# Attention values of a macaron block made in two halves next to fills of transposes

## Chip, core and metric

The kernel runs on one core of a Trainium2 chip. The metric is the device time of one execution in microseconds (us), as the median of several runs. The core's engines are PE (TensorE, the matrix engine), PEld (PE's weight loads, which overlap its matmuls), DVE (VectorE), ACT (ScalarE), POOL (GpSimd) and SP (SyncE, which issues the DMAs here). Each follows its own list of instructions in order and waits on semaphores.

## What is computed

Eight sequences of 512 tokens with 256 channels go through half a feed-forward network, attention with 16 heads of 16 channels and a distance bias, and the same half network again. Everything is float32.

```python
x = x + 0.5 * ffn(layernorm(x))      # silu(x @ wg.T) * (x @ wu.T) @ wd.T, hidden 768
x = x + attention(layernorm(x))
x = x + 0.5 * ffn(layernorm(x))
# attention: B, L, C, H = 8, 512, 256, 16; D = 16
scores = einsum('bhld,bhsd->bhls', qh, kh) * D ** -0.5 - slope[h] * |l - s|
attn = softmax(scores, axis=-1)
out = einsum('bhls,bhsd->bhld', attn, vh)   # then @ Wo.T + bo
```

## The kernel before

There are three stages, each over all eight sequences: the first feed-forward half, attention, and the second half. In the profiled execution attention runs from about 199 to 687 us. The change touches attention alone.

**Steps.** Attention of a sequence b is written out as 4 quads (n = 0 to 3, four heads each) of 8 steps (s = 0 to 7), so 256 steps in all; "step (n, s)" names one. A step deals with one block of 128 keys and one pair of heads. PE makes two score tiles of 512 queries each (`scores`, out of weights `k_aug` and moving `q_aug`), ACT takes the exponential of both at once into `probs` (L656), and POOL multiplies the diagonal block by a table (L525). In every even step PE also makes *values*: `weigh_values` (L1156) multiplies the `probs` of a finished key block, four heads at once in four column strips of 32, with `v_aug` and adds them up in the bank `pv`. The block that an even step takes is two key blocks back, since `probs` has two buffers. The exponentials of an even step go into the buffer which that step's values read, so ACT waits for both `st_done` (the second score tile) and `pv_done` (the values).

**Maxima tiles.** The softmax needs each row's maximum ahead of time. PE makes scores a second time in the other orientation (`scores_for_max`, weights `q_aug`, moving `k_aug`), 64 tiles a sequence, two in each step and 26 tiles ahead, and DVE reduces each (`row_max`, L837). The tiles go in turn to two banks, so a tile waits (`s1_used`) until DVE is through with the tile two before it. A score tile and a maxima tile use different halves of PE's rows. After 16 tiles DVE makes the negated maxima of a quad in two small operations (`max_in`, L847 and L849), and PE transposes them in a later "max" fill; a DMA then brings them to `q_aug`. Where a sequence's list is at its end (the last sequence from step (2, 3) on) there are no tiles.

**Fills.** Every odd step and every step (n, 4) carries a *fill*, a piece of the work on the sequence before, this one or the next, by the table `FILLS`: 8 of the 16 odd steps have four 128-column transposes (`xt`, `turn`, `heads`), the others 6 or 12 matmuls of a projection (`qk`, `v`, `out`), and each (n, 4) the transposes of the maxima. ACT copies a fill's bank to `stage` (L600, L603) or `v_new`, and a next fill waits for that copy. For some of them ACT rounds the copy (L621) and DVE (L893, for `xt`, two steps later) or POOL (L481, for `qk` and `turn`) makes the remainder. DVE also divides the heads (L901, L903), applies layernorms (`apply_kept`, L726) and does the first steps of the last layernorm. All of this stands in each engine's list between the row maxima.

**PE's order in a step** (`turn`): first score tile, first maxima tile, then in an even step the max fill (if s is 4) and the values, in an odd step the fill, then second score tile, second maxima tile. The first score tile of a step waits for the exponentials of two steps before (`exp_done`), whose banks it takes.

## Time and profile before

| | us |
|---|---|
| median of 3 runs | 855.21 (854.73 to 856.42) |
| the profiled execution, device time | 849.82 |
| its span, first to last instruction | 847.9 |
| PE busy | 792.2 (93%) |
| DVE busy | 659.4 (78%) |
| ACT busy | 510.3 (60%) |
| POOL busy | 428.1 (50%) |

Starts of instructions are measured; the ends of matmuls are modelled, and successive matmuls overlap. So PE is read by the distance between starts, not by its busy time. A merged row of the timeline gives the start of the first of its instructions, the time until the last one ends, and their number; two instructions of one engine with the same names stand in one row when nothing else of that engine stands between them. Values are x8 in the trace for four instructions of the program, each of which runs as two.

### The profile page before, as it was taken

To read this page: it belongs to the slowest core of one execution; us is meant where nothing else is said; L and a number is where in the kernel's file an instruction comes from. 1 tells how busy PE (TensorE), PEld (TensorE's weight loads), DVE (VectorE), ACT (ScalarE), POOL (GpSimd) and SP (SyncE) were. 2 spreads that over 40 slices of the span, in tenths; PEclk is the share of its full clock that TensorE was granted. 3 is DMA by queue.
4 is the path that set the end of the run, shared out by engine and by line. 5 is a ranking of instruction groups with operands and counts; after the bars stand their busy time and mean duration, and the time that the engine had idled before them with its cause. 6 is when DMAs were issued, how large, how long until landed. Compare 5 with 4: busy or idle time off the path is not lost.

```text
span 847.9 us, 13038 instructions
## 1 busy us (share of the span) xinstructions
PE 792.2 (93%) x4576; PEld 494.2 (58%) x4576; DVE 659.4 (78%) x1347; ACT 510.3 (60%) x745; POOL 428.1 (50%) x486
## 2 busy tenths in 40 slices
PE   2699999999999999999999999999999799999997
PEld 2478888765444454444454454454453367878886
DVE  6489877977899878978978878878888537677764
ACT  4244354334776877877767777768777774444433
POOL 0244344434564665755755666665664454444433
PEclk9799999998999999999999999999999999999999
DMA  9330005503540540640730720621520000000001
GB/s 362 127 42 3 2 17 78 59 3 43 75 70 9 82 70 3 97 56 2 108 45 7 109 39 19 97 39 32 84 39 2 2 2 27 26 27 28 27 27 51
DMA packets 21491, 43.18 MB, mean 51 GB/s; under 512 B 3848, under 2 KB 5912, under 8 KB 21208
## 3 DMA queue, kind: packets, MB, share of 16 engines
q1 hardware_dynamic: 21400, 41.92, 26.8%
q8 instruction: 63, 1.03, 0.6%
q14 instruction: 28, 0.23, 0.1%
HBM read 12.02 MB, written 4.62 MB: 20 GB/s over the span
## 4 chain that ended last, share of the span: by engine, by line
PE 76%; DVE 17%; issue 3%; DMA 2%; SPq 1%; ACT 1%; DVEq 0%; ACTq 0%
PE ps L970 70%; DVE row_max L837 6%; DVE hid L771 3%; PE ps L1033 2%; DMA q_scale<-q_scale 2%; PE ps L982 1%; DVE max_in L847 1%; DVE max_in L849 1%; DVE newton L703 1%; PE ps L1028 1%; DVE rstd L705 1%; PE ps L1038 1%; PE ps L1008 1%; DVE newton L701 1%; SPq L365 1%
## 5 line engine op out<-in xcount | busy, mean ns | idle before, releaser
L837 DVE TENSOR_REDUCE row_max<-ps 128x1 f32<-128x512 f32 x512 | 331.5, 685 | 72.5 <-PE ps L970 71.6
L656 ACT ACTIVATE probs<-ps 128x1024 f32<-128x1024 f32 x256 | 262.6, 1030 | 84.1 <-PE ps L970 83.3
L525 POOL TENSOR_TENSOR probs<-probs,diag 128x256 f32<-128x256 f32 x256 | 187.8, 734 | 207.2 <-ACT probs L656 205.7
L457 POOL TENSOR_TENSOR hid_r<-hid,hid_r 128x512 fp32r<-128x512 f32 x96 | 124.8, 1301 | 191.0 <-ACT hid_r L551 190.2
L970 PE MATMUL ps<-k_aug,q_aug 60*128 60x512 f32 x512 | 209.8, 470 | 10.9 <-DVE row_max L837 10.2
L970 PE MATMUL ps<-xnt,wgu_r 128*128 128x512 f32 x768 | 193.9, 406 | 18.7 <-DVE hid L771 14.4
L970 PE MATMUL ps<-q_aug,k_aug 62*128 62x512 f32 x512 | 193.4, 454 | 2.7 <-ACT probs L656 2.7
L970 PEld LDWEIGHTS ps<-xnt,wgu_r 128*128 128x128 f32 x768 | 144.2, 192 | 59.6 <-DVE hid L771 19.8
L970 PEld LDWEIGHTS ps<-q_aug,k_aug 62*128 62x128 f32 x512 | 80.6, 186 | 141.7 <-issue 123.9
L970 PE MATMUL ps<-probs,v_aug 128*32 128x512 f32 x1024 | 137.1, 608 | 0.0
L557 ACT ACTIVATE gated<-ps 128x512 f32<-128x512 f32 x96 | 57.3, 598 | 131.2 <-PE ps L970 121.8
L970 PEld LDWEIGHTS ps<-k_aug,q_aug 60*128 60x128 f32 x512 | 84.7, 185 | 40.6 <-DVE row_max L837 30.3
L771 DVE SCALAR_TENSOR_TENSOR hid<-ps,gated 128x512 f32<-128x512 f32 x96 | 65.8, 687 | 46.4 <-ACT gated L557 23.9
L970 PE MATMUL ps<-wdn_r,hid_r 128*128 128x256 f32 x768 | 97.6, 283 | 2.3 <-ACT stage L603 2.3
L970 PEld LDWEIGHTS ps<-wdn_r,hid_r 128*128 128x128 f32 x768 | 93.5, 188 | 5.2 <-ACT hid_r L551 3.2
L551 ACT CAST hid_r<-hid 128x512 fp32r<-128x512 f32 x96 | 59.0, 615 | 24.3 <-DVE hid L771 24.3
L603 ACT COPY stage<-ps 128x512 f32<-128x512 f32 x96 | 56.2, 585 | 20.6 <-PE ps L970 15.7
L970 PE MATMUL ps<-xnt,wqkv 128*128 128x512 f32 x168 | 46.6, 412 | 0.0
L481 POOL TENSOR_TENSOR parts<-stage,parts 128x512 fp32r<-128x512 f32 x32 | 41.3, 1292 | 0.0
L970 PEld LDWEIGHTS ps<-probs,v_aug 128*32 128x32 f32 x1024 | 20.2, 108 | 32.0 <-issue 24.5
L675 DVE BATCH_NORM_STATS2 stats<-x_sb 128x6 f32<-128x256 f32 x96 | 34.1, 409 | 5.3 <-DMA x_sb<-x_in 5.3
L712 DVE TENSOR_SCALAR xn<-x_sb,mean_var,rstd 128x256 f32<-128x256 f32 x64 | 37.7, 614 | 0.5
(72 smaller groups left out, 670.7 us busy)
## 6 DMA issues: line engine op xcount, KB each, us to landing
q_aug<-parts SPq DMA_DIRECT2D x96, 128.0 KB, 4.5
k_aug<-parts SPq DMA_DIRECT2D x96, 128.0 KB, 4.7
x_sb<-x_in SPq DMA_DIRECT2D x8, 512.0 KB, 12.9
x_out<-x_sb SPq DMA_DIRECT2D x8, 512.0 KB, 2.6
diag<-diag_table SPq DMA_DIRECT2D x1, 2048.0 KB, 18.8
wgu_i<-w_gate_up SPq DMA_DIRECT2D x2, 768.0 KB, 6.1
w_att<-w_att SPq DMA_DIRECT2D x1, 1024.0 KB, 11.3
q_aug<-max_row SPq DMA_DIRECT2D x64, 8.0 KB
```

The source lines that it names most:

```text
L457: nc.gpsimd.tensor_tensor(hid_r[:, 1, f, :], hid[:, f % 2, :], hid_r[:, 0, f, :].bitcast(F32), ALU.subtract).then_inc(s["hid_lo"], 1)
L481: nc.gpsimd.tensor_tensor(lo, stage[:, slot_of(b, name), :], hi.bitcast(F32), ALU.subtract).then_inc(done[SPLIT_POOL], 1)
L525: nc.gpsimd.tensor_tensor(tile, tile, diag[:, kt % 2, n * QH + 2 * pair:n * QH + 2 * pair + 2, :], ALU.mult).then_inc(fixed, 1)
L551: nc.scalar.copy(hid_r[:, 0, f, :], hid[:, f % 2, :]).then_inc(s["hid_hi"], 1)
L557: nc.scalar.activation(gated[:, f % 2, :], ps[:, gate_at + f % 2, :], ACT.Silu, scale=DEQ).then_inc(s["gated_ready"], 1)
L603: nc.scalar.copy(stage[:, slot_of(b, name), :], bank).then_inc(drained, 1)
L656: nc.scalar.activation(probs[:, kt % 2, 2 * pair:2 * pair + 2, :], ps[:, at:at + 2, :], ACT.Exp, scale=SLOPE_UNITS[pair]).then_inc(exp_don ...
L675: nc.vector.bn_stats(stats[:, slot, tile, :], x_of(b, tile)).then_inc(ln_step, 1)
L712: nc.vector.tensor_scalar(xn[:, tile, :], x_of(b, tile), mean_var[:, 0, tile, 0:1], rstd[:, 0, tile:tile + 1], ALU.subtract, ALU.mult).the ...
L771: nc.vector.scalar_tensor_tensor(hid[:, f % 2, :], ps[:, up_at + f % 2, :], DEQ, gated[:, f % 2, :], ALU.mult, ALU.mult).then_inc(s["hid_r ...
L837: nc.vector.reduce_max(row_max[:, quad % 2, i, pair, t:t + 1], max_bank(tile), mybir.AxisListType.X).then_inc(s1_used, 1)
L970: return nc.tensor.matmul(out, lhs, rhs, start=start, stop=stop, **k)
```

## The change

An even step that has maxima tiles and whose next step carries a fill of transposes by the table (`xt`, `turn` or `heads`) now makes its values in two parts. Queries 0 to 255 of all four heads come where the values stood. Then come the second score tile and the second maxima tile. Queries 256 to 511 follow after them, at the end of the step, and `pv_done` is raised by these alone. The bank is opened for accumulation by the first part of a quad's first block. These are steps 0, 2 and 4 of quad 0, steps 0 and 4 of quads 1 and 2, and step 4 of quad 3. In the first sequence two of the eight have no values, in the last one two have no tiles, so 60 steps are split. Other engines' programs are the same.

```diff
+TURNS = ("xt", "turn", "heads")
...
-            def weigh_values(quad_no, quad, kt, seq):
+            def weigh_values(quad_no, quad, kt, seq, cols=((0, L),)):
...
-                for g in range(QH):
-                    ins = matmul(pv[32 * g:32 * g + 32, :], v_aug[:, kt, quad * QH + g, :], probs[:, kt % 2, g, :],
-                                 kt == 0, kt == TT - 1, skip_group_check=True)
-                ins.then_inc(pv_done, 1)
+                for lo, hi in cols:
+                    for g in range(QH):
+                        ins = matmul(pv[32 * g:32 * g + 32, lo:hi], v_aug[:, kt, quad * QH + g, :],
+                                     probs[:, kt % 2, g, lo:hi], kt == 0 and lo == 0, kt == TT - 1, skip_group_check=True)
+                if cols[-1][1] == L:
+                    ins.then_inc(pv_done, 1)
...
+                            in_halves = tiles and FILLS[n, s + 1].startswith(TURNS)
                             if s >= 4:
-                                weigh_values(quad_no, n, (s - 4) // 2, b)
+                                values = (quad_no, n, (s - 4) // 2, b)
                             elif not (first(b) and n == 0):
-                                weigh_values(quad_no - 1, (n - 1) % NQ, s // 2 + 2, b)
+                                values = (quad_no - 1, (n - 1) % NQ, s // 2 + 2, b)
+                            else:
+                                values = ()
+                            if values:
+                                weigh_values(*values, ((0, L // 2),) if in_halves else ((0, L),))
...
                         if tiles:
                             scores(b, n, s, 1).then_inc(st_done, 1)
                         scores_for_max(b, tiles[1:])
+                        if s % 2 == 0 and in_halves and values:
+                            weigh_values(*values, ((L // 2, L),))
```

The first place is PE's list at step (1, 0) and the start of step (1, 1) of a sequence. Scores are printed as `ps<-q_aug,k_aug`, maxima tiles as `ps<-k_aug,q_aug`, values as `ps<-probs,v_aug`. Before:

```order
L970 MATMUL ps<-k_aug_86,q_aug_61 128x512 [waits s1_used]
L970 MATMUL ps<-probs,v_aug 32x512 [waits fixed]
L970 MATMUL ps<-probs,v_aug 32x512 x3
L970 MATMUL ps<-q_aug_61,k_aug_86 128x512
L970 MATMUL ps<-k_aug_86,q_aug_61 128x512 [waits s1_used]
L970 MATMUL ps<-q_aug_61,k_aug_86 128x512 [waits exp_done]
L970 MATMUL ps<-k_aug_86,q_aug_61 128x512 [waits s1_used]
L1038 MATMUL ps<-eye,heads 128x128 [waits heads_done,drained]
```

And now:

```order
L972 MATMUL ps<-probs,v_aug 32x256 x3
L972 MATMUL ps<-q_aug_61,k_aug_86 128x512
L972 MATMUL ps<-k_aug_86,q_aug_61 128x512 [waits s1_used]
L972 MATMUL ps<-probs,v_aug 32x256 [waits fixed]
L972 MATMUL ps<-probs,v_aug 32x256 x3
L972 MATMUL ps<-q_aug_61,k_aug_86 128x512 [waits exp_done]
L972 MATMUL ps<-k_aug_86,q_aug_61 128x512 [waits s1_used]
L1040 MATMUL ps<-eye,heads 128x128 [waits heads_done,drained]
```

The four matmuls of 512 columns have become two groups of four with 256, and the second group stands between the second maxima tile of the step and the first score tile of the next.

The second place is PE's list at step (0, 4), from the maxima's transposes to the first of step (0, 5). Before:

```order
L1028 MATMUL ps<-eye,max_in 32x128 [waits neg_ready,drained]
L970 MATMUL ps<-probs,v_aug 32x512 [waits heads_t_ready,v_ready,fixed]
L970 MATMUL ps<-probs,v_aug 32x512 x3
L970 MATMUL ps<-q_aug_60,k_aug_64 128x512
L970 MATMUL ps<-k_aug_86,q_aug_61 128x512 [waits s1_used]
L970 MATMUL ps<-q_aug_60,k_aug_64 128x512 [waits exp_done]
```

And now:

```order
L1030 MATMUL ps<-eye,max_in 32x128 [waits neg_ready,drained]
L972 MATMUL ps<-probs,v_aug 32x256 [waits heads_t_ready,v_ready,fixed]
L972 MATMUL ps<-probs,v_aug 32x256 x3
L972 MATMUL ps<-q_aug_60,k_aug_64 128x512
L972 MATMUL ps<-k_aug_86,q_aug_61 128x512 [waits s1_used]
L972 MATMUL ps<-probs,v_aug 32x256 [waits heads_t_ready,v_ready,fixed]
L972 MATMUL ps<-probs,v_aug 32x256 x3
L972 MATMUL ps<-q_aug_60,k_aug_64 128x512 [waits exp_done]
```

The same split stands behind the transposes of the maxima, whose own waits have not moved.

## Rows read from the trace of the kernel before

**Rows 1.** The page's part 4: the chain that ended last, by line.
```profile
PE ps L970 70%; DVE row_max L837 6%; DVE hid L771 3%; PE ps L1033 2%; DMA q_scale<-q_scale 2%; PE ps L982 1%; DVE max_in L847 1%; DVE max_in L849 1%; DVE newton L703 1%; PE ps L1028 1%; DVE rstd L705 1%; PE ps L1038 1%; PE ps L1008 1%; DVE newton L701 1%; SPq L365 1%
```
**Rows 2.** Busy time of each engine in sequences 1 to 5 (PE, PEld, DVE, ACT, POOL).
```profile
261.00:570.00 309.00, 304.68 (x1826) 149.41 (x1828) 258.60 (x432) 231.97 (x321) 188.10 (x241) 1.00 0.36 53
```
**Rows 3.** Timeline of PE, sequence 3, steps (1, 0) to (1, 2): start, time, instruction.
```profile
399.48 0.40 PE L970 MATMUL ps<-q_aug,k_aug 62*128 62x512 f32 x1
399.81 1.06 PE L970 MATMUL ps<-probs,v_aug 128*32 128x512 f32 x8
400.80 0.49 PE L970 MATMUL ps<-q_aug,k_aug 62*128 62x512 f32 x1
...
401.14 0.39 PE L970 MATMUL ps<-q_aug,k_aug 62*128 62x512 f32 x1
401.48 0.66 PE L1038 MATMUL ps<-eye,heads 128*128 128x128 f32 x4
402.06 0.49 PE L970 MATMUL ps<-q_aug,k_aug 62*128 62x512 f32 x1
...
402.45 0.46 PE L970 MATMUL ps<-q_aug,k_aug 62*128 62x512 f32 x1
402.71 0.50 PE L970 MATMUL ps<-k_aug,q_aug 60*128 60x512 f32 x1
403.14 1.07 PE L970 MATMUL ps<-probs,v_aug 128*32 128x512 f32 x8
...
404.48 0.40 PE L970 MATMUL ps<-q_aug,k_aug 62*128 62x512 f32 x1
```
**Rows 4.** The same timeline, the second four of the values from 399.81 alone.
```profile
400.26 0.61 PE L970 MATMUL ps<-probs,v_aug 128*32 128x512 f32 x4
```
**Rows 5.** Timeline of DVE beside rows 3.
```profile
399.71 1.29 DVE L837 TENSOR_REDUCE row_max<-ps 128x1 f32<-128x512 f32 x2 [0.75 <-PE ps L970]
401.37 2.57 DVE L837 TENSOR_REDUCE row_max<-ps 128x1 f32<-128x512 f32 x4 [0.37 <-PE ps L970]
```
**Rows 6.** Timeline of DVE, sequence 3, steps (0, 5) and (0, 6).
```profile
393.51 1.29 DVE L837 TENSOR_REDUCE row_max<-ps 128x1 f32<-128x512 f32 x2 [0.43 <-PE ps L970]
394.72 1.14 DVE L893 TENSOR_TENSOR xnt<-stage,xnt 128x512 fp32r<-128x512 f32 x1
395.78 2.56 DVE L837 TENSOR_REDUCE row_max<-ps 128x1 f32<-128x512 f32 x4
```
**Rows 7.** Timeline of ACT at step (0, 5), which starts at 393.29.
```profile
393.48 1.02 ACT L656 ACTIVATE probs<-ps 128x1024 f32<-128x1024 f32 x1 [0.44 <-PE ps L970]
```
**Rows 8.** Timeline of POOL behind it.
```profile
394.58 0.72 POOL L525 TENSOR_TENSOR probs<-probs,diag 128x256 f32<-128x256 f32 x1 [0.95 <-ACT probs L656]
```
**Rows 9.** Timeline of PE at the end of step (0, 6).
```profile
396.28 0.49 PE L970 MATMUL ps<-q_aug,k_aug 62*128 62x512 f32 x1
396.51 0.50 PE L970 MATMUL ps<-k_aug,q_aug 60*128 60x512 f32 x1
```
**Rows 10.** Timeline of DVE in the first stage, two small operations.
```profile
81.94 0.16 DVE L719 TENSOR_SCALAR kept_mean<-mean_var 128x4 f32<-128x4 f32 x1
82.01 1.28 DVE L719 TENSOR_SCALAR kept_rstd<-rstd 128x4 f32<-128x4 f32 x1
```
**Rows 11.** Timeline of POOL beside them.
```profile
81.98 1.28 POOL L457 TENSOR_TENSOR hid_r<-hid,hid_r 128x512 fp32r<-128x512 f32 x1
```
**Rows 12.** Timeline of DVE, sequence 3, steps (1, 3) and (1, 4).
```profile
405.43 0.48 DVE L847 TENSOR_SCALAR max_in<-row_max 128x16 fp32r<-128x16 f32 x1
...
408.40 0.58 DVE L726 TENSOR_SCALAR xn<-x_sb,kept_mean,kept_rstd 128x256 f32<-128x256 f32 x1
```
**Rows 13.** Timeline of POOL beside rows 12.
```profile
404.52 1.34 POOL L481 TENSOR_TENSOR att_t<-stage,att_t 128x512 fp32r<-128x512 f32 x1
...
408.78 1.33 POOL L481 TENSOR_TENSOR parts<-stage,parts 128x512 fp32r<-128x512 f32 x1
```
**Rows 14.** Timeline of PE, sequence 3, step (2, 4).
```profile
422.98 0.50 PE L970 MATMUL ps<-k_aug,q_aug 60*128 60x512 f32 x1 [0.50 <-DVE row_max L837]
```

## The prediction

> **What bounds the kernel now.** I read the chain of waits first: 70% of the span lies on PE's matmuls, and the row maxima of DVE hold 6%, the largest share of another engine's line [rows 1]. The busy times of sequences 1 to 5 say the same: in 309 us PE is busy 304.7, DVE 258.6, ACT 232.0, POOL 188.1 [rows 2]. A sequence takes 309/5 = 61.8 us. PE's busy time hides short waits, so I went to the distances between starts, in a step pair that the change touches [rows 3].
>
> Step (1, 0) runs freely. First score tile to values is 0.33 us (399.48 to 399.81), values to second score tile 0.99 (to 400.80), and from there to the next step 0.34: 1.66 in all. The transposes of step (1, 1) take 0.58 (401.48 to 402.06), and with two tile pairs of 0.335 that step would last 1.25. It lasts 1.31 (401.14 to 402.45), since its second maxima tile comes 0.05 late. Step (1, 2) lasts 2.03 (to 404.48) where 1.66 was free: its first maxima tile starts at 402.71, 0.26 behind its score tile, and the values stand 0.43 behind that tile, not 0.33.
>
> DVE explains this [rows 5]. Four row maxima in one run take 2.57 us, so they stand (2.57 - 0.69)/3, about 0.62 us, apart, and a bank is free 0.74 after its row maximum starts. The tiles come unevenly: two within 0.34 us around each step's border, and none for 1.33 while values run. DVE is idle 0.37 before the run and then cannot keep up with four tiles in a row. The wait behind transposes is thus one of rhythm. 8 steps of a sequence are like (1, 1). Free work adds up to about 56 us a sequence (16 even steps of 1.66, four transposes of maxima at 0.3, 16 pairs of tile pairs, and the fills), so waits are about 5.7.
>
> **The split itself.** The second four of the values start 0.45 behind the first (399.81 to 400.26, [rows 4]), and the next tile 0.54 behind them [rows 3]. 512 columns in two passes at 2.4 GHz are 0.427, so 0.026 and 0.115 are not streaming. A half costs 0.213 + 0.026 + 0.213 + 0.115 = 0.57, two halves 1.14 against 0.99. That is **+0.14 us in each of 60 steps, +8.5 us**, all on PE's path. No row shows a 256-column half. Below, the bound is proportion: 0.50 a half and nothing added. Above, I take the first transpose in rows 3, which costs about 0.06 more than the others (0.58 for four at about 0.11, plus the drain): with that at every half it is 0.63, +0.26 a step, +15.8 us. I take 0.57, since all its terms stand around the same instructions.
>
> The split has four changes between tile pairs and values where there were two. I charge one more, since two tile pairs that follow each other also stand 0.34 apart (400.80 to 401.14), 0.12 above 512 columns [rows 3]: the change in front of values costs nothing that a tile pair would not. The Trainium skill, in "TensorEngine Tiling (Array Packing)", section "Key Properties", says that changing the tiling mode drains TensorE, whatever comes next. By that rule two changes are new, with the row's 0.115 each an estimate of +0.26 a step, and the whole change would bring about 1 us; that time is rival D's.
>
> **What the halves give back.** With 0.57 the tiles of a split step come at 0, 0.90, of the next at 1.87, 2.79, of the one after at 3.12. I followed DVE's queue: a row maximum starts 0.56 after its tile's start or 0.61 after the one before; a tile waits until 0.74 after the start of the one two before. Then step (1, 0) lasts 1.875 (its second maxima tile waits 0.07 for a bank), step (1, 1) 1.25, step (1, 2) 1.725 (first maxima tile 0.055 late). Sum 4.85 against 5.00: **a gain of 0.14 to 0.15**, made of -0.22, +0.06 and +0.30. Beside (n, 4) in quad 3 the bank wait is absent and it is 0.23.
>
> ACT's exponential of a split step now waits for the second half. In PE's trace values end modelled 1.06 after their start, 0.07 behind the next score tile's start; ACT starts some 0.04 later, 0.11 into the next step, where it was 0.19 [rows 7]. Its 1.03 us end at 1.14, before step (1, 2) wants the bank at 1.25. No cost, with 0.07 to spare.
>
> **Give-backs, quad by quad.** *Quad 1*: at (1, 3) and (1, 4) POOL holds DVE up. The small `max_in` takes 0.48 where it needs 0.17, until POOL's operation ends at 405.86 [rows 12, 13]. POOL follows ACT, which moves little, so the 0.30 won at (1, 2) comes back at (1, 4) as 0.28 (its first maxima tile 0.80 late, not 0.52). With two gains of 0.15 and 0.22, I get +0.08. *Quad 2*: POOL is without a gap from (2, 1) to (2, 4); the maxima tile at 422.98 stands 0.89 into its step [rows 14], and keeps its absolute place. +0.21. *Quad 3*: +0.23. *Quad 0*: (0, 0) to (0, 2) are even (4.99 before and after). Step (0, 4) gets 0.24 longer: `xnt` (L893) of step (0, 3) is asked for at 1.30, POOL's multiplication starts at 1.21, and DVE stays behind it as now. Step (0, 5) gains 0.06. There the second `xnt` takes 1.14 us today, from 394.72, because POOL began at 394.58 [rows 6, 8], and the next row maximum slips to 395.78; PE's second maxima tile at (0, 6) starts 0.23 behind its score tile [rows 9] and 0.25 more are lost in (0, 7). After the change DVE has no backlog: row maximum at 0.565, `xnt` at 1.165, and POOL at 0.11 + 1.10 = 1.21 (exponential to POOL is 1.10 in rows 7 and 8). DVE is first by 0.05, and steps (0, 6) and (0, 7) come to 1.725 and 2.27 in place of 2.25 and 2.62. Quad 0: **+0.75**.
>
> A sequence wins 0.75 + 0.08 + 0.21 + 0.23 = 1.27; five of them 6.35. Sequence 6 is busier on DVE behind quad 0: 0.9. Sequence 7, tiles until (2, 2): 0.4. Sequence 0, without three of the transposes: 0.4. **Sum: -8.1 us**, net of the +8.5. From the profiled execution, 849.8, that gives 841.7. The runs' median is 5.4 above that execution, and I subtract from the median: **847.1 us**.
>
> **Rivals.** *A. POOL is first at (0, 5).* Its lead is decided by 0.05 us, from distances each good to 0.03. For DVE first: the operation at 81.94 ran in 0.16 though POOL started 0.04 behind it, while the one at 82.01, 0.03 behind POOL, took 1.28 [rows 10, 11]. So the earlier start wins, by whatever margin. Against: recorded starts of DVE overlap the instruction before by 0.08. Then quad 0 gives -0.12, a sequence 0.40, the whole about -2.6: 852.6 us. The Trainium skill, in "SBUF — State Buffer", section "Who interferes with whom", has the same rule: issue order decides, the second fully blocks, and a DVE operation with two SBUF inputs counts. By it the price is this one and no partial slowing.
>
> *B. A dear half.* The split costs more than it gives back. Each of 60 steps gives (8.1 + 8.5)/60 = 0.28 us before its cost, so the result turns slower from a half of 0.64 on (0.50 + 0.14). At 0.66, as if each half paid the 0.06 of a first transpose and the drain of a change at both ends, it is +0.18 a half-pair over my sum, +11: 858 us. For it: no row has column strips of 256. Against: the fixed terms in rows 3 and 4 are measured on these strips.
>
> *C. Two missed gaps.* A, and at (1, 4) the layernorm `xn` (L726) misses the gap between POOL's two operations. Today it is asked for at 408.40, and POOL's next, of 1.33, starts at 408.78 [rows 12, 13]; I put the request 0.10 ahead of that start. If missed, DVE waits 1.3 and 0.66 of the gain in (1, 5) and (1, 6) goes. A sequence then loses 0.26, the whole about 1.5: 856.7 us, measured the same or slower.
>
> *D. The change does little*: with two new drains, a half of 0.63, its effects nearly cancel, 8.1 - 60 x 0.115 = 1.2 us faster: 854.0. Against it stand the equal distances of rows 3.
>
> **How the numbers follow.** Forecast 0.42; A 0.24; B 0.11; C 0.11; D 0.12. A measurement of this kernel can tell about 0.2%, 1.7 us, from no change. Faster by more: the forecast, most of A (0.21) = 0.63, and a little of C's weaker form 0.02: 0.65. Within: 0.12 + 0.03 + 0.05 = 0.20. Slower: 0.11 + 0.04 = 0.15. Range: at its low end the forecast with a half of 0.54 (3.6 us less), 843.5; at its high end A and D and the mild form of C, 856.5.
>
> **What would show it.** In the profile after: (1) distance between the two starts of a half and the score tile behind it, 0.57; (2) steps (1, 0), (1, 1), (1, 2) of 1.87, 1.25, 1.73; (3) exponential of a split step 0.11 into the next; (4) at (0, 5) `xnt` in about 0.6 us and POOL's multiplication behind it, steps (0, 6) and (0, 7) of 1.73 and 2.27; (5) the first maxima tile of (1, 4) about 0.80 late; (6) a sequence of about 60.5 us. Wrong would be a half above 0.64, or `xnt` still at 1.1 us in (0, 5), or PE waiting for `exp_done` behind the transposes.

## Result: the changed kernel is slower

| | before | after |
|---|---|---|
| median, us | 855.21 (854.73 to 856.42) | 864.33 (863.43 to 865.05) |
| ratio after/before, 95% interval | | 1.0116 [1.0087, 1.0145] |
| profiled execution / its span, us | 849.82 / 847.9 | 864.14 / 862.4 |
| granted clock of PE, mean over the span | 0.990 | 0.974 |

The change costs 1.2%. The forecast was 847.1 us with a range of 843.5 to 856.5: wrong in sign, and the time is outside the range. Two executions far above all others are in no median: one of the kernel before (1718 us) and one of the run `q0_fed` below (1054 us, mean granted clock 0.644).

From the profile of the changed kernel, the busy us and share by engine, and the granted clock in 40 slices, in tenths:

```profile
PE 801.2 (93%) x5056; PEld 499.4 (58%) x5056; DVE 662.7 (77%) x1347; ACT 511.4 (59%) x745; POOL 434.1 (50%) x486
PEclk9799999997998999999999999999999799999999
```

The chain that ended last has hardly changed: PE's matmuls hold 69% of it and the row maxima 5%, against 70% and 6% in [rows 1]. The row of clocks has three dips inside attention (slices 10, 13 and 32, counted from 1) where before's profiled execution has one. (The dip in slice 2 stands in the first feed-forward half, in both kernels.) Next, the busy times by stretch (window, length, busy us of PE, PEld, DVE, ACT, POOL with counts; granted clock, DMA share, GB/s). The stretches are sequence 0, sequences 1 to 5, sequence 6, and sequence 7 to the last step. Before:

```profile
198.60:260.60 62.00, 58.82 (x314) 27.23 (x313) 53.64 (x111) 42.00 (x56) 30.75 (x41) 0.94 0.48 67
260.60:569.40 308.80, 304.48 (x1821) 149.57 (x1822) 258.45 (x433) 231.77 (x320) 188.04 (x241) 1.00 0.36 53
569.40:632.70 63.30, 62.34 (x366) 30.92 (x365) 54.42 (x107) 46.79 (x65) 37.70 (x49) 1.00 0.35 52
632.70:685.30 52.60, 46.41 (x277) 19.20 (x273) 31.41 (x55) 39.49 (x52) 27.89 (x37) 1.00 0.01 2
```

After:

```profile
198.70:266.40 67.70, 63.74 (x361) 28.91 (x361) 53.71 (x111) 42.17 (x56) 30.72 (x41) 0.85 0.43 61
266.40:576.20 309.80, 303.16 (x2143) 151.55 (x2142) 261.56 (x433) 232.54 (x320) 192.28 (x241) 1.00 0.35 53
576.20:640.40 64.20, 62.10 (x432) 31.04 (x428) 55.08 (x107) 46.64 (x65) 38.53 (x49) 1.00 0.35 51
640.40:698.70 58.30, 52.00 (x325) 20.64 (x321) 31.84 (x55) 39.56 (x52) 28.68 (x37) 0.88 0.01 2
```

The 14.5 us between the two profiled spans are +5.7 in sequence 0, +1.0 in sequences 1 to 5, +0.9 in sequence 6, +5.7 in sequence 7 and +1.2 outside. So there are two separate results. Sequences 1 to 5 run at full clock in both and lose 1.0 us where 6.35 were to be won. Sequences 0 and 7 hold 12 of the 60 split steps and lose 11.4 us, with the granted clock down from 0.94 to 0.85 and from 1.00 to 0.88.

**Inside a step.** The timeline of PE in sequence 3, steps (1, 0) to (1, 2) of the changed kernel (start, time, instruction, count; compare [rows 3]):

```profile
405.74 0.39 PE L972 MATMUL ps<-q_aug,k_aug 62*128 62x512 f32 x1
406.06 0.64 PE L972 MATMUL ps<-probs,v_aug 128*32 128x256 f32 x8
406.63 0.49 PE L972 MATMUL ps<-q_aug,k_aug 62*128 62x512 f32 x1
406.71 0.49 PE L972 MATMUL ps<-k_aug,q_aug 60*128 60x512 f32 x1
407.13 0.64 PE L972 MATMUL ps<-probs,v_aug 128*32 128x256 f32 x8
407.70 0.50 PE L972 MATMUL ps<-q_aug,k_aug 62*128 62x512 f32 x1
...
408.13 0.66 PE L1040 MATMUL ps<-eye,heads 128*128 128x128 f32 x4
408.71 0.50 PE L972 MATMUL ps<-q_aug,k_aug 62*128 62x512 f32 x1
...
409.06 0.42 PE L972 MATMUL ps<-q_aug,k_aug 62*128 62x512 f32 x1
...
410.75 0.39 PE L972 MATMUL ps<-q_aug,k_aug 62*128 62x512 f32 x1
```

A half takes 0.57 (406.06 to 406.63, 407.13 to 407.70), as forecast. The three steps last 1.96, 1.36 and 1.70, 5.02 together, against 4.85 forecast and 5.00 before. What is longer than forecast is a tile pair that stands alone between two blocks of other work. From the second tile of the pair to the second half are 0.42 (406.71 to 407.13), from the pair of step (1, 1) to the transposes 0.43 (407.70 to 408.13). Both were charged 0.335. No wait is behind this, as steps (3, 4) and (3, 5) of the same sequence show, where the maxima tile starts with its score tile:

```profile
446.52 0.50 PE L972 MATMUL ps<-q_aug,k_aug 62*128 62x512 f32 x1
446.52 0.50 PE L972 MATMUL ps<-k_aug,q_aug 60*128 60x512 f32 x1
446.95 0.64 PE L972 MATMUL ps<-probs,v_aug 128*32 128x256 f32 x8
447.52 0.50 PE L972 MATMUL ps<-q_aug,k_aug 62*128 62x512 f32 x1
447.52 0.49 PE L972 MATMUL ps<-k_aug,q_aug 60*128 60x512 f32 x1
447.95 0.66 PE L1035 MATMUL ps<-eye,heads_t 128*128 128x128 f32 x4
```

Two lone pairs, 0.43 each, both tiles starting together. In the kernel before, as long as there are maxima tiles, a pair always has another behind or ahead of it, and the two take 0.68 together (400.80 to 401.48 in [rows 3]). Where the second of two pairs has its maxima tile late (402.71), from that tile to the values are 0.43 as well: the prediction read that row as rhythm. The end of the last sequence has no maxima tiles, and there the kernel before has lone pairs, of two score tiles. They take 0.43 too:

```profile
672.24 0.50 PE L970 MATMUL ps<-q_aug,k_aug 62*128 62x512 f32 x2
672.67 1.07 PE L970 MATMUL ps<-probs,v_aug 128*32 128x512 f32 x8
```

**What a lone pair pays for.** 0.43 us would be 512 columns in two passes at 2.4 GHz, so a lone pair might simply stream that long. The trace of the kernel before says no. Six matmuls of 512 columns of a projection fill, declared with the same data type as the tiles (`F32R`), take 1.58 from the first to the next score tile:

```profile
404.81 1.65 PE L970 MATMUL ps<-xnt,wqkv 128*128 128x512 f32 x6
406.39 0.49 PE L970 MATMUL ps<-q_aug,k_aug 62*128 62x512 f32 x1
```

One takes 0.43, two in a row 0.67 to 0.68, six 1.58: 0.23 to 0.25 for each one more, and about 0.2 once for the whole run. 0.213 is one pass of 512 columns at 2.4 GHz. At half clock (rows of sequence 7 of the changed kernel) a lone pair takes 0.72 and two in a row 1.15:

```profile
665.58 0.79 PE L972 MATMUL ps<-q_aug,k_aug 62*128 62x512 f32 x1
666.30 1.11 PE L1035 MATMUL ps<-eye,heads_t 128*128 128x128 f32 x4
667.35 0.79 PE L972 MATMUL ps<-q_aug,k_aug 62*128 62x512 f32 x1
...
668.50 1.93 PE L972 MATMUL ps<-probs,v_aug 128*32 128x512 f32 x8
```

The second pair adds 0.43, which is one pass at 1.2 GHz, while two passes would make the lone pair 0.85. So the tiles stream once, and some 0.2 us (0.3 at half clock) are paid once for every unbroken run, at its ends. Where one kind of matmul follows another and both use the whole array, in the first stage, no such price shows. The next row counts the last four of a 512-column projection, and the kind behind them starts 0.94 later, 0.235 for each of the four:

```profile
60.38 1.10 PE L970 MATMUL ps<-xnt,wgu_r 128*128 128x512 f32 x4
61.32 0.28 PE L970 MATMUL ps<-wdn_r,hid_r 128*128 128x256 f32 x1
```

In 20 of the 22 changes between two projections in that stage the distances are like that. A single maxima tile between two projections takes 0.42 to 0.43 there in all 12 places, though its data type is theirs. The price thus goes with the change between the whole array and a part of it, and a split adds one run of tiles and one of values. (A change to transposes, which are of another data type, adds about 0.1 in that stage without a change of tiling, so the data type may hold a part of the price beside values or transposes.)

**Quad by quad.** Sequence 3, from the start of each quad's first step, in us:

| quad | before | after | change | forecast | forecast + 0.19 for each split step |
|---|---|---|---|---|---|
| 0 (3 split steps) | 15.16 | 14.79 | -0.37 | -0.75 | -0.18 |
| 1 (2) | 15.33 | 16.00 | +0.67 | -0.08 | +0.30 |
| 2 (2) | 15.75 | 15.67 | -0.08 | -0.21 | +0.17 |
| 3 (1) | 15.46 | 15.44 | -0.02 | -0.23 | -0.04 |

The last column adds two lone pairs of 0.43 - 0.335 = 0.095 to each split step. It accounts for quad 3. Quads 0 and 2 come out about 0.2 better than it, quad 1 is 0.37 worse. That the four together fit, +0.20 measured and +0.25 in the last column, is partly luck. The reason for quad 1 stands in DVE's timeline at step (1, 4):

```profile
414.96 1.52 DVE L728 TENSOR_SCALAR xn<-x_sb,kept_mean,kept_rstd 128x256 f32<-128x256 f32 x1
```

and in POOL's beside it:

```profile
415.05 1.28 POOL L483 TENSOR_TENSOR parts<-stage,parts 128x512 fp32r<-128x512 f32 x1
```

The layernorm `xn` starts at 414.96, 0.09 (from unrounded starts 0.084) ahead of POOL's `parts` at 415.05, takes 1.52 and ends 0.15 behind it. In [rows 12] it took 0.58, and POOL's operation started 0.38 behind it [rows 13]. In sequence 4 of the same execution it came through:

```profile
476.87 0.41 DVE L728 TENSOR_SCALAR xn<-x_sb,kept_mean,kept_rstd 128x256 f32<-128x256 f32 x1
```
```profile
476.97 1.44 POOL L483 TENSOR_TENSOR parts<-stage,parts 128x512 fp32r<-128x512 f32 x1
```

The recorded lead is 0.10 there. It is 0.08 in the four sequences that missed, and 0.07 to 0.09 in the five of run `mid` below, which all missed. Quad 1 took 15.62 in the sequence that came through and 16.00 to 16.03 in 1, 2, 3 and 5. So to be first in the records is not enough; with a single one that came through, where the border lies isn't known.

At (0, 5) DVE is first, as the forecast had it:

```profile
401.44 0.68 DVE L895 TENSOR_TENSOR xnt<-stage,xnt 128x512 fp32r<-128x512 f32 x1
```

POOL's multiplication follows at 401.58, and the operation takes 0.68 in place of 1.14 [rows 6].

**The clock.** PE in sequence 7, steps (1, 3) and (1, 4) of the changed kernel:

```profile
661.07 0.46 PE L972 MATMUL ps<-q_aug,k_aug 62*128 62x512 f32 x1
662.74 0.50 PE L972 MATMUL ps<-k_aug,q_aug 60*128 60x512 f32 x1 [1.22 <-DVE row_max L839]
...
664.57 1.08 PE L972 MATMUL ps<-probs,v_aug 128*32 128x256 f32 x8
```

And the busy times just before and after 664.1:

```profile
657.30:664.10 6.80, 5.22 (x35) 2.27 (x34) 5.84 (x9) 5.23 (x8) 4.10 (x5) 1.00 0.00 0
664.10:670.90 6.80, 6.80 (x30) 2.44 (x32) 2.67 (x4) 2.64 (x3) 1.45 (x2) 0.50 0.01 2
```

Sequence 7 has little beside its own steps: its list has no `qk` and `v` fills, and at (1, 4) PE waits for DVE. PE is busy 5.22 of 6.80 us, then the granted clock is 0.50 (1.2 GHz in place of 2.4), and the same eight matmuls of 256 columns take 1.08 where they took 0.64. Sequence 0, which has no `turn` or `heads` of a sequence before, has such stretches too. In the changed kernel's profiled execution attention holds four of them (from 203.3, 257.9, 664.1 and 681.2 us, 34 us together), in before's one, at 203.5, of 6.8 us. The Trainium skill's page "TensorE: Matmul & The Clock Gate" names the behaviour in its section "HAM oscillation — how this bites in real kernels"; it says that waits make the clock fall and that the work behind them starts slow, at a penalty of half the throttled time. This stretch agrees on the first, but waits alone don't decide it: in before's profiled execution PE is busy 15.56 of the 20 us from 660 us on, about the same share, and the clock stays at 1.00. On the second, an estimate by that page would be 0.5 us for each us at half clock; the executions below show 0.38.

**Half-clock time.** Each execution comes with its span and mean granted clock, so its time at half clock is 2 x (1 - clock) x span. That is 43 us for the changed kernel (41 to 45 in its four executions) and 17 in before's profiled one. It differs between executions of the same kernel, as the next section shows, and everything from here on is read with it.

### The profile page after: what moved, and what is told of

The parts are those of the page before. It is cut to its first block, busy times and chain, and to the rows that moved or that the text cites. A ratio compares the mean times of both kernels' runs of the same rounds, so it can differ in the third digit from the quotient of the medians.

```text
span 862.4 us, 14028 instructions
## 1 busy us (share of the span) xinstructions
PE 801.2 (93%) x5056; PEld 499.4 (58%) x5056; DVE 662.7 (77%) x1347; ACT 511.4 (59%) x745; POOL 434.1 (50%) x486
## 3 DMA queue, kind: packets, MB, share of 16 engines
q8 instruction: 66, 1.08, 0.6%
## 4 chain that ended last, share of the span: by engine, by line
PE 75%; DVE 15%; issue 4%; DMA 2%; ACT 2%; SPq 1%; DVEq 0%; ACTq 0%
PE ps L972 69%; DVE row_max L839 5%; DVE hid L773 3%; PE ps L1035 2%; DMA q_scale<-q_scale 2%; PE ps L984 1%; DVE newton L705 1%; DVE max_in L851 1%; DVE max_in L849 1%; PE ps L1040 1%; DVE xn L728 1%; PE ps L1030 1%; ACT probs L658 1%; DVE rstd L707 1%; PE ps L1010 1%
## 5 line engine op out<-in xcount | busy, mean ns | idle before, releaser
L839 DVE TENSOR_REDUCE row_max<-ps 128x1 f32<-128x512 f32 x512 | 335.9, 685 | 79.5 <-PE ps L972 78.3
L527 POOL TENSOR_TENSOR probs<-probs,diag 128x256 f32<-128x256 f32 x256 | 193.5, 756 | 214.8 <-ACT probs L658 213.0
L972 PE MATMUL ps<-k_aug,q_aug 60*128 60x512 f32 x512 | 214.8, 480 | 11.7 <-DVE row_max L839 11.6
L972 PE MATMUL ps<-q_aug,k_aug 62*128 62x512 f32 x512 | 206.7, 473 | 3.5 <-ACT probs L658 3.4
L972 PEld LDWEIGHTS ps<-q_aug,k_aug 62*128 62x128 f32 x512 | 85.3, 189 | 145.9 <-issue 129.0
L972 PE MATMUL ps<-probs,v_aug 128*32 128x256 f32 (+1 forms) x1504 | 154.7, 484 | 0.0
L972 PEld LDWEIGHTS ps<-k_aug,q_aug 60*128 60x128 f32 x512 | 89.4, 187 | 29.7 <-DVE row_max L839 26.2
L972 PEld LDWEIGHTS ps<-probs,v_aug 128*32 128x32 f32 x1504 | 29.9, 109 | 48.4 <-issue 39.5
## 6 DMA issues: line engine op xcount, KB each, us to landing
w_att<-w_att SPq DMA_DIRECT2D x1, 1024.0 KB, 10.7
```

The lines of the kernel that those rows point to most:

```text
L527: nc.gpsimd.tensor_tensor(tile, tile, diag[:, kt % 2, n * QH + 2 * pair:n * QH + 2 * pair + 2, :], ALU.mult).then_inc(fixed, 1)
L839: nc.vector.reduce_max(row_max[:, quad % 2, i, pair, t:t + 1], max_bank(tile), mybir.AxisListType.X).then_inc(s1_used, 1)
L972: return nc.tensor.matmul(out, lhs, rhs, start=start, stop=stop, **k)
```

## Experiments

The runs were made in three batches, each beside its own executions of the kernel before. "At 17" is the value at 17 us of half-clock time on a straight line through all executions of that kernel, time against half-clock time. The slopes of these lines are 0.19 to 0.44. With 0.38 for all, the values move by at most 1.4 us (`ends` 852.1, `end7` 850.5, `late` 870.7), so "at 17" is good to about 1 us.

| kernel | median us (range, executions) | half-clock us, median | at 17 | ratio to before, 95% |
|---|---|---|---|---|
| before, batch 1 | 854.18 (848.33 to 859.56, 35) | 22 | 851.3 | |
| same | 853.64 (847.44 to 857.5, 12) | 21 | 851.4 | 0.9984 [0.9949, 1.0019] |
| mid | 855.66 (850.59 to 859.82, 12) | 22 | 852.8 | 1.0003 [0.9969, 1.0036] |
| ends | 860.82 (851.96 to 862.9, 12) | 40 | 851.4 | 1.0053 [1.0021, 1.0085] |
| adjacent | 850.39 (848.66 to 857.14, 12) | 15 | 851.1 | 0.9961 [0.9934, 0.9989] |
| before, batch 2 | 853.74 (847.66 to 860.09, 29) | 20 | 851.1 | |
| after_fed | 861.74 (852.51 to 864.51, 11) | 34 | 855.3 | 1.0071 [1.0036, 1.0107] |
| before_fed | 849.28 (847.81 to 852.31, 12) | 10 | 850.8 | 0.9978 [0.9949, 1.0007] |
| mid_apply | 851.77 (848.49 to 857.63, 12) | 21 | 850.8 | 0.9995 [0.9961, 1.0029] |
| late | 879.20 (872.59 to 882.84, 3) | 39 | 869.4 | 1.0298 [1.0231, 1.0366] |
| before, batch 3 | 854.44 (848.84 to 857.51, 33) | 21 | 852.6 | |
| q0_fed | 847.89 (846.53 to 848.96, 9) | 15 | 848.3 | 0.9933 [0.9908, 0.9957] |
| end0 | 854.20 (850.29 to 860.63, 12) | 24 | 851.5 | 1.0013 [0.9985, 1.0040] |
| end7 | 854.85 (851.88 to 861.13, 12) | 31 | 851.9 | 1.0011 [0.9986, 1.0037] |
| adjacent_all | 851.58 (850.22 to 854.7, 12) | 18 | 851.7 | 0.9976 [0.9956, 0.9997] |

### The kernel before, beside itself

No edit: the kernel before under a name of its own.

> The kernel before, submitted against itself, to see the granted clock of each execution. Theory (half-clock stretches): an execution with clock 0.99 in the mean takes about 850 us, and those near 855 us show a lower mean clock, since 6.8 us at half speed on a busy PE cost about 3.4 us. Rival (the 5.4 us between the profiled execution and the median have nothing to do with PE's clock): clock 0.99 in all of them. Ratio 1.000 either way.

Its twelve executions run from 847.44 to 857.5 us, a spread of 1.2%. In order of half-clock time (us of time / us at half clock): 847.4/10, 848.1/10, 849.4/10, 849.5/10, 853.0/19, 854.3/19, 852.2/24, 855.6/26, 854.8/31, 856.7/32, 857.1/33, 857.5/33. The line has a slope of 0.36 us for each us at half clock (0.38 in before's 35 executions), and leaves 1.2 us (one standard deviation) unexplained. So most of this kernel's scatter goes with the clock. It also explains about half of the 5.4 us by which the profiled execution of before, 849.8, lay under its median of 855.2. It had 17 us at half clock, where 22 are usual and 39 the most, and the line is at 851.3 there, 2.9 under the median of the 35. Of the rest, 1.0 is that the median of the first three was high (854.2 in the 35), and 1.5 is scatter.

### Splits in the middle, splits at the ends

`mid` splits the 48 steps of sequences 1 to 6, `ends` the 12 of sequences 0 and 7.

```diff
-                            in_halves = tiles and FILLS[n, s + 1].startswith(TURNS)
+                            in_halves = tiles and FILLS[n, s + 1].startswith(TURNS) and 0 < b < B - 1
```
```diff
+                            in_halves = tiles and FILLS[n, s + 1].startswith(TURNS) and b in (0, B - 1)
```

> The split in sequences 1 to 6 alone, 48 steps. Theory (the loss is half-clock time in the first and last sequence, where fills are missing): those two are as before, sequences 1 to 5 take 0.2 us more each and sequence 6 about 0.9, so 1.5 to 2.5 us over the kernel before, with no half-clock stretch beyond its own. Rival (the split costs about the same in each of the 60 steps): 48/60 of 9.1, so 7.3 us over.

> The split in sequences 0 and 7 alone, 12 steps, the complement of the run before. Theory (half-clock time): 7 to 12 us over the kernel before, with four half-clock stretches in attention, 34 us in all. Rival (cost per step): 12/60 of 9.1, so 1.8 us over.

`ends` is the slower of the two with a quarter of the splits: +6.6 us by the medians. Nearly all of it comes with half-clock time, 40 us against 22. At equal half-clock time it is within 1 us of before (851.4 against 851.3). Its profiled execution has three low stretches in attention, not the four expected: before's one at 203 us and two more, of 6.8 and 13.6 us, both in sequence 7. Its stretch of sequence 7:

```profile
643.00:699.00 56.00, 50.61 (x281) 20.29 (x282) 25.67 (x46) 35.25 (x45) 25.82 (x33) 0.82 0.01 2
```

`mid` has before's half-clock time, and is 1.5 us slower at equal half-clock time. The medians differ by 1.5 too, though the ratio's interval holds 1. That is the 1.5 to 2.5 expected; 7.3 would lie outside the interval. In the profiles sequences 2 to 5 take 61.9 each, against 61.7. The low clock isn't confined to the two ends: the profiled execution of `mid` has a stretch of it in sequence 6, which before's has not, and quad 1 takes 19.20 there against 16.26 in the changed kernel:

```profile
571.00:638.00 67.00, 64.72 (x432) 31.66 (x428) 55.48 (x107) 46.78 (x65) 38.39 (x49) 0.95 0.32 49
```

### One end alone

```diff
+                            in_halves = tiles and FILLS[n, s + 1].startswith(TURNS) and b == 0
```
```diff
+                            in_halves = tiles and FILLS[n, s + 1].startswith(TURNS) and b == B - 1
```

> The split in sequence 0 alone (6 steps). Theory (clock): half-clock time rises over the kernel before's 20 to 22 us by what the changed kernel has more in sequence 0, up to 14 us, and the time goes along with 0.35 to 0.4 us for each: 855 to 860 us. Rival (steps in sequence 0 cost by themselves): 6 x 0.1 us, no more half-clock time.

> The split in sequence 7 alone (6 steps). Theory (clock): half-clock time rises by up to 14 us, 855 to 860 us, and together with end0 the two rises add up to that of run ends, 18 us in the median. Rival: no more half-clock time, 0 to 1 us slower.

Both medians, 854.20 and 854.85, stay under the 855 to 860 expected. The means rise by only 0.9 and 1.3 us over before's, those of `ends` by 5.9. Mean half-clock times rise by 5 and 7 us, those of `ends` by 13, so the clock's part about adds up. At the slope of 0.38 these are 2 and 3 us, and `end0` and `end7` come out about 1 us better at equal half-clock time than before in that batch. That before is itself 1.3 us higher at 17 than in the two other batches. I take this for the limit of what such comparisons settle, about 1 us.

### Values in two groups, but in one place

`adjacent` makes the two halves of the 60 steps one behind the other where values stood before. `adjacent_all` does so in every even step.

```diff
-                                weigh_values(*values, ((0, L // 2),) if in_halves else ((0, L),))
+                                weigh_values(*values, ((0, L // 2), (L // 2, L)) if in_halves else ((0, L),))
...
-                        if s % 2 == 0 and in_halves and values:
-                            weigh_values(*values, ((L // 2, L),))
```

> All 60 steps make values in two groups of 256 columns, but both where the values stood, with nothing between them. Theory (what costs is a lone pair of tiles between two changes of tiling, and the clock follows idle time, not short matmuls): values take 1.04 us instead of 0.995, PE's other distances are as before, no new half-clock stretch; 0 to 3 us over the kernel before. Rival (256 columns in strips are what costs): as the changed kernel, 9 us over.

> Values in two groups of 256 columns with nothing between them in all even steps, also those next to other fills (run adjacent had it in 60 steps, and had less half-clock time than the kernel before in its 12 executions, 15 against 22 us in the median). If twice as many, shorter matmuls keep the clock up, the half-clock time is again at 10 to 16 us and the time 849 to 851. If that was chance, 20 to 22 us and 854 again.

PE at step (1, 0) of `adjacent`:

```profile
399.14 1.07 PE L972 MATMUL ps<-probs,v_aug 128*32 128x256 f32 x16
400.14 0.50 PE L972 MATMUL ps<-q_aug,k_aug 62*128 62x512 f32 x1
```

1.00 for sixteen records of 256 columns against 0.99 for eight of 512 [rows 3]: less than the 1.04 expected. The width of the groups costs nothing; all that a split costs is in leaving and coming back. Both kernels stand within 1 us of their batch's before at equal half-clock time (851.1 against 851.3, 851.7 against 852.6), and yet their medians are 3.8 and 2.9 us under it, with 15 and 18 us at half clock. The 18 us and 851.6 of `adjacent_all` lie between the two cases of its expectation (10 to 16 us, or 20 to 22). That these kernels meet the low clock less often is measured, why is not known.

### Values whole, behind the second maxima tile

`late` makes the values of the 60 steps whole, in the place of the second half. Each split step then has three tile pairs on one side and one on the other.

```diff
-                            if values:
-                                weigh_values(*values, ((0, L // 2),) if in_halves else ((0, L),))
+                            if values and not in_halves:
+                                weigh_values(*values)
...
-                            weigh_values(*values, ((L // 2, L),))
+                            weigh_values(*values)
```

> In all 60 steps the values are made whole, behind the second maxima tile. Theory (a lone pair of tiles between two blocks of other tiling takes 0.43 us, two pairs in a row 0.67): values take 0.995 again, the pair in a split step costs 0.335 each, the pair between values and the transposes 0.43, so step (1, 0) is 1.66 and (1, 1) 1.36 us. Rival (the 0.43 belongs to 256-column groups): the pair behind whole values takes 0.335, step (1, 1) 1.25 to 1.31. For the time each expects about the kernel before, since DVE's tiles come in pairs again, plus the exponential's later start.

PE at steps (1, 0) and (1, 1):

```profile
408.93 0.49 PE L972 MATMUL ps<-k_aug,q_aug 60*128 60x512 f32 x1 [0.35 <-DVE row_max L839]
409.35 1.06 PE L972 MATMUL ps<-probs,v_aug 128*32 128x512 f32 x8
410.35 0.49 PE L972 MATMUL ps<-q_aug,k_aug 62*128 62x512 f32 x1
410.77 0.66 PE L1040 MATMUL ps<-eye,heads 128*128 128x128 f32 x4
```

The lone pair behind values takes 0.42 here too (410.35 to 410.77), though these values are whole: the price belongs to standing alone, not to halves. But step (1, 0) is 2.39 long, where 1.66 was expected. Three maxima tiles in a row meet two banks, and PE waits for DVE, 0.35 at the tile of 408.93. At equal half-clock time the kernel is about 18 us slower (three executions). My expectation had counted PE's instructions and not DVE's rhythm.

### The gap of `xn`

`mid` again, with the second part of the kept layernorm one step later.

```diff
-APPLY_AT = {(1, 2): 0, (1, 4): 1, (1, 6): 2, (2, 2): 3}
+APPLY_AT = {(1, 2): 0, (1, 5): 1, (1, 6): 2, (2, 2): 3}
```

> The split in sequences 1 to 6, as in run mid, with DVE's layernorm of one tile (line 728) moved from step (1, 4) to (1, 5). Theory (the missed gap between two POOL operations at (1, 4) costs quad 1 its 0.67): quad 1 of sequences 1 to 5 takes 15.3 to 15.4 us in place of 16.02, and the whole is 3 to 4 us under run mid at the same half-clock time. Rival (quad 1 loses by PE's extra time in its two split steps): quad 1 stays within 0.1 of 16.0.

DVE's `xn` in `mid`, then in `mid_apply`:

```profile
409.33 1.52 DVE L728 TENSOR_SCALAR xn<-x_sb,kept_mean,kept_rstd 128x256 f32<-128x256 f32 x1
```
```profile
410.76 0.41 DVE L728 TENSOR_SCALAR xn<-x_sb,kept_mean,kept_rstd 128x256 f32<-128x256 f32 x1
```

Quad 1 of sequence 3 goes from 16.04 to 15.62, of the others in the same way. So the missed gap costs 0.42 a sequence, not the 0.66 of rival C, and the quad doesn't come down to the 15.3 to 15.4 expected. The 0.29 left over before's 15.33 are what two split steps with their lone pairs come to in the table above (0.30). The whole comes 2.0 us under `mid` at equal half-clock time, under the 3 to 4 expected, though the two are of different batches. Five times 0.42 are 2.1: sequence 6 has no such layernorm, and its quad 1 takes 16.26 in `mid_apply` as in the changed kernel.

### Work that nobody reads

`before_fed` and `after_fed` are the kernels before and after, with four transposes of the unit matrix in the 11 odd steps of sequences 0 and 7 that have no fill. They go to the fills' bank and are never read.

```diff
+            def idle_work(b, n, s):
+                done_fills = [(c, f) for c, f in IN_ORDER if c < b] + [
+                    (b, f) for at, f in FILLS.items() if at < (n, s) and f in fills_of(b)]
+                wait(pe, drained, len(done_fills))
+                for t in range(TT):
+                    nc.tensor.transpose(ps[:, misc, t * P:(t + 1) * P], eye[:], eye[:])
...
+                        elif name:
+                            idle_work(b, n, s)
```

> The kernel before with the same 11 groups of idle transposes. Theory (clock): half-clock time falls from 22 us in the median to 10 to 17, 2 to 4 us faster than the kernel before. Rival (PE's path): 0 to 6 us slower.

> The changed kernel, and in the 11 odd steps of the first and last sequence whose fill is missing PE makes four 128-column transposes of a constant that nobody reads. Theory (the half-clock stretches come where PE has little to do, and cost 0.38 us for each us of them): PE gets more work and the kernel gets faster; half-clock time falls from 43 us an execution to under 30, the time from 864.3 to 860 or less. Rival (PE's own path is what counts, the clock is incidental): up to 11 x 0.6 us slower, 865 to 871.

Before with this work has 10 us at half clock in most executions (10 to 20; without it 10 to 43), and its median falls by 4.5 us, to 849.28, with a narrower range. Its sequence 7:

```profile
632.00:684.50 52.50, 48.73 (x301) 21.32 (x299) 31.37 (x54) 39.45 (x52) 27.80 (x37) 1.00 0.01 2
```

PE is busy 48.7 us against 46.4 of the same 52.5: the added transposes stand in time that PE waited anyway. The ratio, 0.9978, has an interval that still holds 1, as the executions of before beside it scatter over 12 us; the two medians have a ratio of 0.9948.

In the changed kernel the cure is partial. Its executions fall into two groups, 10 to 24 and 34 to 36 us at half clock, with a median of 861.74. At equal half-clock time it stands 4 us over before. In its profiled execution (21 us at half clock) the low clock holds 10.2 us from 203 us on and 3.4 in sequence 6, from 599 us. Where the executions with 34 to 36 have theirs no run shows.

### Only the quad that gains

Quad 0 alone won something in the changed kernel, -0.37 a sequence. `q0_fed` splits the 18 steps of quad 0 in sequences 1 to 6 and has the idle transposes.

```diff
+                            in_halves = tiles and FILLS[n, s + 1].startswith(TURNS) and n == 0 and 0 < b < B - 1
```

> The split in quad 0 of sequences 1 to 6 alone (18 steps), where the quads of run mid were 0.37 us shorter than before, together with the 11 groups of idle transposes of run before_fed. Theory: half-clock time as in before_fed (10 to 13 us), quads 0 at 14.77 in place of 15.15, so 6 x 0.37 = 2.2 us under before_fed: 847 us, 0.6 to 0.9% under the kernel before. Rival (the gain of quad 0 is taken back later in the sequence, as a DVE or POOL backlog): quads 1 longer by as much, 849 us.

The median is 847.89 us, 0.9933 [0.9908, 0.9957] of before: faster than both kernels, and 1.4 us under `before_fed`. The quads of sequence 3 take 14.74, 15.33, 15.74 and 15.43: the 0.4 of quad 0 stays won, as it was not in the changed kernel, whose quad 1 gave it back. One sequence:

```profile
384.80:446.00 61.20, 60.11 (x392) 29.58 (x388) 51.37 (x87) 46.43 (x65) 38.44 (x49) 1.00 0.35 54
```

61.2 against 61.7, at full clock. Sequences 2 to 5 win 0.4 each, sequence 6 wins 0.2 and sequence 1 nothing (quad 0 takes 15.50 and 15.48 there), 1.8 us in all. At equal half-clock time `q0_fed` is 2.5 under `before_fed` (848.3 against 850.8), though the two are of different batches, so the 1.4 and the 2.5 are good to 1 us or so; the 1.8 are read inside one trace each.

## Why the prediction was wrong

**The price of a half** was right: 0.57 forecast, 0.57 measured, and rival B's 0.64 and more did not come.

**A tile pair costs 0.335 wherever it stands** is the step that turned the sign of the sum. The words were "the change in front of values costs nothing that a tile pair would not". A pair alone between two other blocks takes 0.43, two in a row 0.68. A split step makes two lone pairs out of pairs that stood in twos, so 0.19 is missing in each, 60 x 0.19 = 11.4 us in all. The sum of -8.1 becomes +3.3 by that alone. For sequences 1 to 6 the sum so mended gives -7.25 + 48 x 0.19 = +1.9, and the profiles show +1.9 (1.0 and 0.9), though part of that is luck, as the quads show. The row was there: in [rows 3] the values stand 0.43 behind the maxima tile at 402.71, and I took the distance for a wait that the change would remove. The lone pairs of score tiles at the end of sequence 7 (672.24) had the price plainly, and I read no row there. The rule of the Trainium skill ("TensorEngine Tiling (Array Packing)", section "Key Properties") that every change of the tiling mode drains TensorE pointed in this direction. I had given it 0.115 a step as rival D, and a chance of 0.12; the runs show 0.19 and where it lies. The rows under "What a lone pair pays for" agree with the rule: about 0.2 us for every run between two changes of the tiling, and nothing between two kinds of matmul that both use the whole array. Before the change these ends were paid too; what the prediction missed is that the split makes one run of tiles more, whose ends cost as much as those of a long one.

**The gap of `xn`** was rival C's, and happened while DVE was still first at (0, 5), which rival C had tied to rival A for no reason of its own. The first maxima tile of (1, 4) comes 0.82 late where 0.80 was forecast, and `xn` starts 0.09 ahead of POOL where 0.10 was. The arithmetic was right; what failed is the rule, taken in rival A from [rows 10, 11], that the earlier start wins by whatever margin. It costs 0.42 a sequence (`mid_apply` against `mid`) in the sequences where it happens.

**Give-backs.** Step (1, 2) is 1.70 (forecast 1.725), and `xnt` at (0, 5) takes 0.68. The steps behind it, 1.70 and 2.40, were forecast at 1.725 and 2.27. The four changes that the prediction lists for quad 0 (-0.24, +0.06, +0.525, +0.35) add up to 0.70, not 0.75, which is a slip. At (0, 3) DVE was first too (`xnt` at 397.43, POOL at 397.56), where it was to stay behind POOL, and step (0, 4) takes 2.67 against 2.66 before, not the 0.24 more that were forecast. That is more than the 0.19 by which quad 0 beats its corrected forecast. In sequence 1 quad 0 won nothing at all (15.49 against 15.48), which I had not looked at. The exponential of a split step starts 0.20 into the next step, not 0.11, with no wait of PE for it behind the transposes:

```profile
407.90 1.02 ACT L658 ACTIVATE probs<-ps 128x1024 f32<-128x1024 f32 x1 [0.28 <-PE ps L972]
```

**The clock** has no term in the prediction at all, and it is the largest part of the result. Against before's 35 executions of batch 1 (mean 853.6 at 23 us of half-clock time), the changed kernel's four (864.3 at 43) are 10.7 us slower. 20 us x 0.38 = 7.6 of that go with half-clock time, the other 3 are about what the step times come to. `ends` shows where the 7.6 come from: 12 splits in sequences 0 and 7 raise half-clock time by 18 us at the median. [rows 2] covers sequences 1 to 5, which run at 1.00, and I read nothing of the clock in the two sequences where PE has time to spare. I also took the distance of 5.4 between the profiled execution and the median as a constant. It was chance, some 3 us of it in step with the half-clock time (17 us in that execution, 22 in the usual one). The prediction's claim that 0.2% can be told from no change didn't hold either, as single executions of the kernel before range over 1.3%.

**Still open.** By extrapolation the changed kernel is 3 us above before at equal half-clock time, `mid` and `ends` together only 1.5; four executions, all between 41 and 45 us at half clock, don't settle which. Open too is why `end0` and `end7` together cost less than `ends`, why adjacent groups meet the low clock less often, and what makes it fall in one execution and not in the next.

## To carry to other kernels

Read distances between blocks by their neighbours: the price of a short block is the one it has between the neighbours it will get, and cutting a block in two may isolate others. Count the runs of like matmuls before and after a reordering. Where PE has stretches with waits, put the granted clock into the sum, and compare executions at equal half-clock time, since a kernel's own scatter (1.2% here in twelve executions) may be larger than the change. Work that nobody reads can hold the clock up at no cost, where PE would wait anyway (`before_fed`; in the changed kernel it did so in part of the executions); and a reordering should be kept only in the place where the trace shows its gain stays, here one quad of four.

## What the hardware showed that was not expected

- The same kernel takes 847.4 to 857.5 us in twelve executions, with 10 to 33 us at half clock; each us at half clock goes with about 0.38 us of time.
- Values in groups of 256 columns cost as much as in 512 (1.00 against 0.99 us for the same work) when nothing stands between them.
- A pair of 512-column tiles takes 0.43 us alone and 0.68 for two in a row, and six 512-column matmuls of the same type 1.58: about 0.2 us is paid once for a run between two changes of the tiling, and none shows between two kinds that both use the whole array.
- `xn` on DVE took 0.41 us with a recorded lead of 0.10 us over POOL's operation, and 1.50 to 1.52 in nine cases with one of 0.07 to 0.09. A forecast of who is first can't be made to 0.1 us.
